# A two-layer graph network: layer one's turns written out, layer two's weights scaled and composed earlier

## The chip, the cores and the metric

The kernel runs on 1 core of one Trainium2 chip. The metric is the device time of one execution in microseconds (us); the figure compared is the median over runs.

## The reference

The input is a graph with 3125 nodes of 160 features (64 scalars and 32 three-vectors) and 103125 edges, sorted by the node that they point to. Two layers follow each other. Each normalises the node features (`h = max(layernorm(x), 0)`), gathers `h` of each edge's source node, forms a message from it and the edge's four attributes, sums the messages of each target node, and adds the result to `x`.

```python
# layer one (edge_scalars: 64 per edge, fc_w1, fc_w2: the edge's own weights)
w = silu(edge_scalars @ fc_w1 * c) @ fc_w2 * c          # 224 weights for each edge
m = products of w, (h @ lin1)[src] and the edge's attributes e0, e1
agg = segment_sum(m, dst)                               # to the target nodes
pre = (h @ sc) + (agg @ lin2)                           # scalars and vectors
x = x + [silu(pre_s[:64]), sigmoid(pre_s[64:96]) * pre_v]
# layer two (no weights of the edge's own)
m = h[src] and the edge's attributes, times W1..W5
x = x + relu(segment_sum(m, dst) @ (Ws, Wv))
```

Layer two's W1..W5 and its output weights Ws, Wv are linear, one after the other, so the kernel multiplies them into one set of planes ("composes" them) before it needs them.

## The kernel before

**Tiling.** Nodes lie in 25 tiles of 128. Edges lie in tiles of 128, 7 tiles to a group, 116 groups, 4 groups to a *turn*, 29 turns (`ITERS`) in a layer. A group's place in its turn is `o`, 0 to 3; the group's number is `s`.

**A group of layer one.** The synchronisation engine SP loads the edge features (`load_feat`). TensorE multiplies them with fc1 (`hidden`, L1216), ScalarE applies silu (L920), TensorE multiplies with fc2 (`edge_weights`, L1230). VectorE builds the selection matrices of the group (`select`, L996 and L1000), multiplies the edge weights with the gathered rows `g` (`products`, L1087 to L1105, in two halves h=0 of 4 tiles and h=1 of 3 tiles), and TensorE sums them into a window of 32 target nodes (`aggregate`, L1266). VectorE turns the sums (`turn`, L1112), TensorE multiplies them with the layer's output weights once a turn (`lin2`, L1304), ScalarE copies, VectorE adds into the accumulator at a place read from memory (`accumulate`, L1118 and L1133).

**Where the rows `g` come from.** Most tiles are gathered by POOL, one indirect transfer for each tile (`gather`, L871 to L897). A buffer of `g` is used again one turn later, so a group's gathers wait for the products (layer one) or the aggregation (layer two) of the same group of the turn before. Some tiles are found instead by comparing node numbers on VectorE (L1016, L1051) and multiplying the match with the node table on TensorE (L1287, L1294; joined at L1035, L1060): 2 tiles a turn in layer one, 4 or 5 in layer two. One tile in two of three turns is brought row by row, 128 small transfers with addresses read from memory, by SP (the first of the two) and ScalarE's queue (the second), `fetch_rows`, L779.

**Order of the turns.** `stages` (L732) calls an engine's `stage` for every group. Turns 0 and 1 are written out, turns 2 to 25 are a hardware loop over 8 periods of 3 turns, turns 26 to 28 are written out again. TensorE, VectorE and ScalarE use it in both layers. SP has a loop of its own; POOL's code is written out over all turns. Around all turns lies one more loop (`passes`), run once with these inputs.

**The head.** The node features are normalised and transformed, the table of rows is written to memory in six pieces (L379), POOL gathers the first 7 tiles (L393). SP's last transfers are a load of edge features (L380), the store of `first_rows`, which waits for `first_ready`, and the four transfers of layer two's weights `pair`, `pair_k`, `wout`, `wout_k` (L383 to L386). VectorE's last work of the head is `vector_self`: scaling `big0_sb` (L552), seven copies of TensorE's sums (L555), and the split of the node table in two halves of precision (L558).

**Between the layers.** TensorE transposes layer one's sums tile by tile (L1356), ScalarE makes sigmoid gates (`gate`, L1375), VectorE forms the gated values and the next layer norm's statistics (L1405 to L1421), POOL adds (L1457). VectorE and ScalarE normalise (L1431, L349), SP writes the second table (L1468), the table is split (L1388, L1390, L1443), VectorE computes window indices (L531 to L535). Then VectorE scales layer two's weights (L1448, L1449), TensorE composes them into 5 planes (L1365), ScalarE copies the planes (L1394), casts the first named rows (L935, L941), and VectorE's first comparison of layer two (L1051) follows.

The loop that the change takes away from layer one, as the code has it:

```python
with eng.Fori(0, PERIODS - 1) as k:
    e = eng.snap(PERIODS * r + k)
    for p in range(PERIOD):
        it = eng.snap(PERIOD * k + (LEAD + p))
        f = eng.snap(q + it)
        for o in range(UNROLL):
            stage(f, it, o, None, p, e, k)
```

Of the kernel before, what the change touches and what calls it, by code (L numbers as in the profile page):

```python
# [64 lines left out]


# [23 lines left out]
ROW_TILES = (2, 2)  # L90
PARTS = (48, 48, 32)
# [10 lines left out]
def build(nc, x, node_vec, x_node, src_idx, src_rows0, src_rows1, src_by_row, node_id, dst_idx, edge_sh, edge_feat, ident, iota, lin_sc, lin_sc_scale,  # L102
# [8 lines left out]
    with ctx:  # L111
# [250 lines left out]
        def sync_head(sp):  # L362
# [18 lines left out]
            sp.wait_ge(first_ready, RAW)  # L381
            sp.dma_start(first_rows, g[:, 0:RAW, :].rearrange("p t c -> p (t c)")).then_inc(first_out, 16)
# [3 lines left out]
            sp.dma_start(wout_k[:], l1_out_scale).then_inc(pair_in, 16)  # L386
            sp.sem_inc(first_back, 1)
# [162 lines left out]
        def vector_self(dve):  # L550
            dve.wait_ge(big0_in, 32)
            nc.vector.tensor_tensor(big0_sb[:], big0_sb[:], big0_k, ALU.mult).then_inc(big0_ready, 1)  # L552
            for j, at in enumerate(CHUNK_N):
                dve.wait_ge(sc_done[1], j + 1)
                nc.vector.tensor_copy(acc0[:, 1, at], sums[0:S_OUT, SC_BANK[1][j], 0:at.stop - at.start]).then_inc(sc_ready[1], 1)  # L555
            dve.wait_ge(rows_out, 16 * len(HEAD_PIECES))
            dve.wait_ge(upper0_ready, 2)
            nc.vector.tensor_tensor(split0[:, 0, :, :], H, split0[:, 1, :, :].bitcast(F32), ALU.subtract).then_inc(split0_ready, 1)  # L558
            dve.wait_ge(sc_ready[0], len(CHUNK_N))
            dve.wait_ge(pad_clear, 1)  # L560
            dve.wait_ge(edges_in, 48)
            dve.wait_ge(turns_set, 1)
# [87 lines left out]
        def edge_layer(layer):  # L650
# [81 lines left out]
            def stages(eng, r, stage, last):  # L732
# [4 lines left out]
                q = eng.snap(ITERS * r)  # L737
                e = eng.snap(PERIODS * r + 0) - 1
# [176 lines left out]
            def scalar(act):  # L915
# [30 lines left out]
                def row_part(f, it, o, s, p, e, k):  # L946

                    if ROW_TILES[layer] < 2 or o >= UNROLL or p < -1 or (p == PERIOD - 1 and s is not None):
                        return
# [400 lines left out]

        def tensor_mid(pe):
            for t in range(NT):
                if t >= BANKS:
                    pe.wait_ge(val_ready, t - BANKS + 1)
                for r in range(2):
                    last = nc.tensor.transpose(banks[:, t % BANKS, r * S_OUT:(r + 1) * S_OUT], acc0[:, r, t * P:(t + 1) * P],  # L1356
                                               ident_sb[0:S_OUT, 0:S_OUT])
                last.then_inc(node0_done, 1)
            pe.wait_ge(val_ready, NT)
            pe.wait_ge(weights_ready, 1)  # L1360
            for m in range(PLANES[1]):
                if m >= BANKS:
                    pe.wait_ge(comp_copied, m - BANKS + 1)
                for c in range(2):
                    last = nc.tensor.matmul(banks[:, m % BANKS, 0:D], pair[:, 2 * m + c, :], wout[:, c, :],  # L1365
                                            start=(c == 0), stop=(c == 1))
                last.then_inc(comp_done, 1)
            pe.wait_ge(comp_copied, PLANES[1])

        def scalar_mid(act):  # L1370
# [8 lines left out]
            for t in range(NT):  # L1379
                gate(t)  # L1380
            root(act, parts[0], 0, var1_step, root1_done)
# [10 lines left out]
            for m in range(PLANES[1]):  # L1392
                act.wait_ge(comp_done, m + 1)
                nc.scalar.activation(big1_sb[:, m, :], banks[:, m % BANKS, 0:D], ACT.Copy).then_inc(comp_copied, 1)  # L1394

        def vector_mid(dve):
# [50 lines left out]
            dve.wait_ge(pair_in, 64)  # L1447
            nc.vector.tensor_tensor(pair[:], pair[:], pair_k[:], ALU.mult)  # L1448
            nc.vector.tensor_tensor(wout[:], wout[:], wout_k[:], ALU.mult).then_inc(weights_ready, 1)  # L1449
# [258 lines left out]
```

## Time and profile before

| | |
|---|---|
| median of 3 runs | 1861.78 us (1860.4 to 1862.68) |
| profiled execution | time 1865.19 us, span 1863.4 us |
| busy in the span | PE 1714.3 us (92%), DVE 1685.2 us (90%), POOL 1339.0 us (72%), ACT 171.4 us (9%) |
| head | 0 to about 50 us |
| layer one | about 50 to 982 us |
| between the layers | about 982 to 1028 us |
| layer two and the end | about 1028 to 1863 us |

Names of the profile: PE is TensorE, PEld its weight loads, DVE VectorE, ACT ScalarE, POOL GpSimd, SP the synchronisation engine; a q behind an engine's name is its queue of instructions (transfers and register work). In a timeline a row is: start in us, duration in us, engine, line, operation, written tile and read tiles, shapes, count; in brackets the idle time of the engine just before it and what ended it. "issue" is idle time that nothing in the profile releases. Time in the span is counted from the first instruction.

### The profile page before, as it was taken

The numbers are of one execution on the slowest core, as the hardware profiler recorded it, in microseconds if no ns is written. First come the engines' busy times: TensorE is split into PE (matmuls) and PEld (weight loads), VectorE is DVE, ScalarE is ACT, GpSimd is POOL, SyncE is SP. The second block draws the span as 40 slices with busy tenths as digits, with TensorE's granted clock in tenths as the row PEclk, the third lists the DMA queues.
The fourth block names the chain that finished last, engine by engine and source line by source line (L and its number), as shares of the span: only waits on it lengthen the run. The fifth ranks groups of instructions, "written<-read, shape, count | busy, mean of one in ns | idle before, by whom it ended". The sixth has DMA issues, their size and how long they took to land.

```text
span 1863.4 us, 57341 instructions
## 1 busy us (share of the span) xinstructions
PE 1714.3 (92%) x15973; PEld 1488.8 (80%) x15973; DVE 1685.2 (90%) x3031; ACT 171.4 (9%) x359; POOL 1339.0 (72%) x1424
## 2 busy tenths in 40 slices
PE   8999899989898989999983899999999999999997
PEld 6677676777676767777752899999999999999997
DVE  7999899989999999999988988989898989889896
ACT  6100000000000000000005000000000000000000
POOL 4777777777777777777755777777777777777774
PEclk9899999999999999999995999999999999999999
DMA  8344443443434343434422333333333333333333
GB/s 278 105 106 108 108 110 96 107 106 98 118 91 110 102 109 103 108 91 116 112 75 86 78 84 76 83 75 84 82 76 80 83 75 82 75 81 83 74 84 90
DMA packets 109737, 181.03 MB, mean 97 GB/s; under 512 B 30072, under 2 KB 74480, under 8 KB 109248
## 3 DMA queue, kind: packets, MB, share of 16 engines
q0 software_dynamic: 66672, 113.88, 25.6%
q1 hardware_dynamic: 35592, 60.39, 10.4%
q10 hardware_dynamic: 7112, 2.94, 0.7%
q8 instruction: 106, 1.74, 0.4%
q14 instruction: 255, 2.09, 0.4%
HBM read 170.37 MB, written 6.72 MB: 95 GB/s over the span
## 4 chain that ended last, share of the span: by engine, by line
DVE 36%; PE 28%; issue 23%; ACTq 6%; DVEq 6%; DMA 1%; ACT 0%; POOL 0%; POOLq 0%
PE w_ps L1294 10%; DVE arena L1093 10%; DVE arena L1087 6%; DVE match L1051 5%; ACTq L779 5%; PE sums L1266 3%; PE sums L1270 3%; DVEq L1118 3%; PE sums L1304 3%; DVE mixed L996 3%; PE w_ps L1230 3%; DVE turned L1112 2%; PE hid_ps L1216 2%; DVE arena L1101 2%; DVE sel L1000 1%
## 5 line engine op out<-in xcount | busy, mean ns | idle before, releaser
L894 POOL DMA_INDIRECT g<-node_table,src x1382 | 1314.3, 951 | 462.1 <-issue 405.9
L1294 PE MATMUL w_ps<-split,match 128*128 128x320 f32 x3325 | 531.4, 318 | 7.9 <-DVE match L1051 7.4
L1294 PEld LDWEIGHTS w_ps<-split,match 128*128 128x128 f32 x3325 | 504.0, 193 | 12.0 <-DVE match L1051 12.0
L1051 DVE TENSOR_TENSOR match<-hid_ps,node_id_sb 128x3200 fp32r<-128x3200 f32 x105 | 361.4, 3456 | 6.9 <-ACT hid_ps L935 6.9
L1093 DVE TENSOR_TENSOR arena<-w_ps,g 128x384 f32<-128x384 f32 (+3 forms) x693 | 296.7, 455 | 2.0 <-DMA g<-node_table 1.3
L1266 PEld LDWEIGHTS sums<-arena,sel 128*32 128x32 f32 x6448 | 203.8, 111 | 116.5 <-DVE sel L1000 57.9
L1230 PE MATMUL w_ps<-fc_sb,arena 64*128 64x224 f32 x1612 | 226.9, 382 | 56.2 <-DVE arena L1087 29.5
L1000 DVE TENSOR_TENSOR sel<-mixed,sh 128x896 f32<-128x896 f32 x232 | 251.5, 1084 | 27.2
L1270 PE MATMUL sums<-g,sel 128*128 128x160 f32 x1612 | 241.5, 300 | 24.0 <-DMA g<-node_table 21.9
L1266 PE MATMUL sums<-arena,sel 128*32 128x160 f32 x6448 | 245.8, 303 | 18.0 <-DVE g L1035 17.9
L1270 PEld LDWEIGHTS sums<-g,sel 128*128 128x128 f32 x1612 | 227.2, 190 | 26.6 <-DMA g<-node_table 24.1
L1230 PEld LDWEIGHTS w_ps<-fc_sb,arena 64*128 64x128 f32 x1612 | 167.4, 193 | 100.2 <-DVE arena L1087 56.0
L1287 PE MATMUL sums<-split,match 128*128 128x320 f32 x1350 | 212.6, 313 | 0.0
L1287 PEld LDWEIGHTS sums<-split,match 128*128 128x128 f32 x1350 | 198.4, 188 | 13.6 <-issue 13.6
L1016 DVE TENSOR_TENSOR match<-mixed,node_id_sb 128x3200 fp32r<-128x3200 f32 x54 | 188.1, 3484 | 0.9
L1087 DVE TENSOR_TENSOR arena<-w_ps,g 128x256 f32<-128x256 f32 x462 | 155.6, 376 | 0.0
L1216 PE MATMUL hid_ps<-arena,fc_sb 128*128 128x512 f32 x232 | 136.2, 670 | 1.8 <-issue 1.8
L920 ACT ACTIVATE arena<-hid_ps 128x512 f32<-128x512 f32 x116 | 69.4, 598 | 740.7 <-PE hid_ps L1216 553.2
L996 DVE TENSOR_TENSOR mixed<-mixed,rel 128x224 f32<-128x224 f32 x232 | 89.4, 386 | 37.3 <-issue 30.2
L1112 DVE STREAM_TRANSPOSE turned<-sums 128x160 f32<-128x160 f32 x232 | 78.3, 338 | 26.0 <-PE sums L1304 23.1
L1051 DVE TENSOR_TENSOR match<-mixed,node_id_sb 128x3200 fp32r<-128x3200 f32 x28 | 97.8, 3492 | 1.0
L1060 DVE TENSOR_REDUCE g<-w_ps 128x160 f32<-128x320 f32 x133 | 62.5, 476 | 17.6 <-PE w_ps L1294 17.6
(113 smaller groups left out, 793.0 us busy)
## 6 DMA issues: line engine op xcount, KB each, us to landing
g<-node_table SPq DMA_DIRECT2D x2304, 0.6 KB
g<-node_table ACTq DMA_DIRECT2D x2304, 0.6 KB
arena<-edge_feat_dram SPq DMA_DIRECT2D x60, 512.0 KB
g<-node_table,src POOLq DMA_INDIRECT x1382
named<-src_rows_dram SPq DMA_DIRECT2D x30, 320.0 KB
named<-src_rows_dram SPq DMA_DIRECT2D x30, 128.0 KB
X<-x_dram SPq DMA_DIRECT2D x5, 400.0 KB, 6.5
sh<-edge_sh_dram SPq DMA_DIRECT2D x1, 1624.0 KB, 9.2
```

The costliest lines, as they stand in the source:

```text
L894: nc.gpsimd.indirect_dma_start(out=g[:, slot(p, u, j), :], out_offset=None, in_=table[layer], in_offset=bass.IndirectOffsetOnAxis(ap=src[: ...
L1000: nc.vector.tensor_tensor(sel[:, o % 2, 0:n, :].rearrange("p t (k n) -> p t k n", k=4), hot[:, 0:n, :].unsqueeze(2).to_broadcast([P, n, 4, ...
L1016: nc.vector.tensor_tensor(match0[:], wanted0[:, i, :].unsqueeze(1).to_broadcast(wide), node_id_sb[:].unsqueeze(2).to_broadcast(wide), ALU. ...
L1051: nc.vector.tensor_tensor(match[MATCH_OF[i]][:], wanted_of[i].unsqueeze(1).to_broadcast(wide), node_id_sb[:].unsqueeze(2).to_broadcast(wid ...
L1087: return nc.vector.tensor_tensor(blocks(at), w[:, :, h * S_CH:(h + 1) * S_CH].rearrange("p t (m c) -> p t m c", m=2), rows[:, :, 0:S_CH].r ...
L1093: nc.vector.tensor_tensor(blocks(at), w[:, :, 2 * S_CH + j * V_CH:2 * S_CH + (j + 1) * V_CH].unsqueeze(2).to_broadcast([P, n, m, V_CH]), r ...
L1216: nc.tensor.matmul(hid_ps[:], fc1_sb[:], feat[:, half, within * HID:(within + 1) * HID], start=True, stop=True).then_inc(hid_done, 1)
L1230: last = nc.tensor.matmul(w_ps[:, h, part[2 * h + j] - a, 0:W_N], hid[at, o % 2, (2 * h + j) * P:(2 * h + j + 1) * P], fc2_sb[at, :], tile ...
L1266: last = nc.tensor.matmul(sums[at, o % 2, 0:width].rearrange("p (m n) -> p m n", n=WIN), sel[:, o % 2, j, at], row, tile_position=(0, k * ...
L1270: last = nc.tensor.matmul(sums[:, o % 2, 0:D], sel[:, o % 2, j, :], g[:, slot(p, o % UNROLL, j), :], **first_last)
L1287: last = nc.tensor.matmul(found_at, match0[:, t, :], split0[:, :, t, :], start=(t == 0), stop=(t == NT - 1))
L1294: last = nc.tensor.matmul(banks[:, BANK_OF[i], 0:2 * D], match[MATCH_OF[i]][:, t, :], split[:, t, :], start=(t == 0), stop=(t == NT - 1))
```

## The change

1. `stages` gets a branch for layers listed in `WRITTEN_OUT`, here layer one alone: all 29 turns are written out in the code of TensorE, VectorE and ScalarE, with the turn's number known when the code is made. SP keeps its loop, POOL's code is as it was.
2. SP issues the four transfers of layer two's weights ahead of the wait for `first_ready`.
3. VectorE scales these weights in the head, in `vector_self` behind `big0_sb`, no longer between the layers.
4. TensorE composes a plane after the transposes of tiles 4, 8, 12, 16 and 20 of the stage with the gates, in the two banks of `sums` by turns; ScalarE copies a plane two tiles later, between two gates.
5. The condition in `row_part` that leaves out the last turn is written in another way, with the same effect.

```diff
+COMPOSED_AT = (4, 8, 12, 16, 20)
+WRITTEN_OUT = (0,)
@@ sync_head
             load_feat(sp, 1, 1)
-            sp.wait_ge(first_ready, RAW)
-            sp.dma_start(first_rows, g[:, 0:RAW, :].rearrange("p t c -> p (t c)")).then_inc(first_out, 16)
             sp.dma_start(pair[:], l1_pair).then_inc(pair_in, 16)
             sp.dma_start(pair_k[:], l1_pair_scale).then_inc(pair_in, 16)
             sp.dma_start(wout[:], l1_out).then_inc(pair_in, 16)
             sp.dma_start(wout_k[:], l1_out_scale).then_inc(pair_in, 16)
+            sp.wait_ge(first_ready, RAW)
+            sp.dma_start(first_rows, g[:, 0:RAW, :].rearrange("p t c -> p (t c)")).then_inc(first_out, 16)
@@ vector_self
             nc.vector.tensor_tensor(big0_sb[:], big0_sb[:], big0_k, ALU.mult).then_inc(big0_ready, 1)
+            dve.wait_ge(pair_in, 64)
+            nc.vector.tensor_tensor(pair[:], pair[:], pair_k[:], ALU.mult)
+            nc.vector.tensor_tensor(wout[:], wout[:], wout_k[:], ALU.mult).then_inc(weights_ready, 1)
@@ stages
                 q = eng.snap(ITERS * r)
+                if layer in WRITTEN_OUT:
+                    for it in range(ITERS):
+                        f = eng.snap(q + it)
+                        k, p = divmod(it - LEAD, PERIOD) if it >= LEAD else (-1, it - LEAD)
+                        e = eng.snap(PERIODS * r + max(k, 0)) - (it < LEAD)
+                        for s in range(UNROLL * it, UNROLL * (it + 1) if it < ITERS - 1 else last):
+                            stage(f, it, s - UNROLL * it, s, p, e, k)
+                    return
@@ row_part
-                    if ROW_TILES[layer] < 2 or o >= UNROLL or p < -1 or (p == PERIOD - 1 and s is not None):
+                    if ROW_TILES[layer] < 2 or o >= UNROLL or p < -1 or isinstance(it, int) and it == ITERS - 1:
@@ new functions
+        def compose(pe, m):
+            if m == 0:
+                pe.wait_ge(weights_ready, 1)
+            if m >= 2:
+                pe.wait_ge(comp_copied, m - 1)
+            for c in range(2):
+                last = nc.tensor.matmul(sums[:, m % 2, 0:D], pair[:, 2 * m + c, :], wout[:, c, :], start=(c == 0), stop=(c == 1))
+            last.then_inc(comp_done, 1)
+
+        def composed(act, m):
+            act.wait_ge(comp_done, m + 1)
+            nc.scalar.activation(big1_sb[:, m, :], sums[:, m % 2, 0:D], ACT.Copy).then_inc(comp_copied, 1)
@@ tensor_mid, in the loop over the 25 tiles
+                if t in COMPOSED_AT:
+                    compose(pe, COMPOSED_AT.index(t))
@@ tensor_mid, behind it
-            pe.wait_ge(weights_ready, 1)
-            for m in range(PLANES[1]):
...
-                last.then_inc(comp_done, 1)
@@ scalar_mid
             for t in range(NT):
                 gate(t)
+                if t - 2 in COMPOSED_AT:
+                    composed(act, COMPOSED_AT.index(t - 2))
...
-            for m in range(PLANES[1]):
-                act.wait_ge(comp_done, m + 1)
-                nc.scalar.activation(big1_sb[:, m, :], banks[:, m % BANKS, 0:D], ACT.Copy).then_inc(comp_copied, 1)
@@ vector_mid
-            dve.wait_ge(pair_in, 64)
-            nc.vector.tensor_tensor(pair[:], pair[:], pair_k[:], ALU.mult)
-            nc.vector.tensor_tensor(wout[:], wout[:], wout_k[:], ALU.mult).then_inc(weights_ready, 1)
```

## Rows read from the trace of the kernel before

**Rows 1.** Timeline, VectorE, first selection of turns 2, 5, 6 and 26.

```profile
114.57 0.40 DVE L996 TENSOR_TENSOR mixed<-mixed,rel 128x224 f32<-128x224 f32 x1 [0.33 <-PE sums L1266]
...
213.12 0.40 DVE L996 TENSOR_TENSOR mixed<-mixed,rel 128x224 f32<-128x224 f32 x1 [3.64 <-issue]
...
244.81 0.40 DVE L996 TENSOR_TENSOR mixed<-mixed,rel 128x224 f32<-128x224 f32 x1 [0.18 <-PE sums L1266]
...
897.17 0.40 DVE L996 TENSOR_TENSOR mixed<-mixed,rel 128x224 f32<-128x224 f32 x1
```

**Rows 2.** Timeline, TensorE, at a return of the loop.

```profile
206.98 1.77 PE L1230 MATMUL w_ps<-fc_sb,arena 64*128 64x224 f32 x14 [3.07 <-issue]
```

**Rows 3.** Busy times by stretch: turn 26 of layer one; three turns of layer two.

```profile
core 0: us, PE busy (x) PEld busy (x) DVE busy (x) ACT busy (x) POOL busy (x), PEclk, DMA share, GB/s
897.17:928.20 31.03, 29.39 (x355) 22.79 (x355) 30.55 (x70) 2.77 (x5) 23.41 (x26) 1.00 0.39 108
1146.32:1232.47 86.15, 83.03 (x579) 82.30 (x579) 77.53 (x80) 3.54 (x9) 65.09 (x70) 0.98 0.32 81
```

**Rows 4.** Timeline, POOL, layer one; the last is its last gather.

```profile
349.19 0.95 POOL L894 DMA_INDIRECT g<-node_table,src  x1 [0.74 <-issue]
...
415.91 0.94 POOL L894 DMA_INDIRECT g<-node_table,src  x1 [3.23 <-DVE arena L1087]
...
961.53 0.95 POOL L894 DMA_INDIRECT g<-node_table,src  x1 [0.30 <-issue]
```

**Rows 5.** Waits from 311 to 897 us: total, times, longest.

```profile
POOL g L894 <- DVE arena L1087: 18.8, 18, 3.2
```

**Rows 6.** Page, transfers: KB each, median us to landing.

```profile
wout_k<-l_out_scale_dram SPq DMA_DIRECT2D x1, 160.0 KB, 8.5
...
arena<-x_node_dram,src POOLq DMA_INDIRECT x7, 3.7
```

**Rows 7.** Timeline, VectorE, products of group 113, second half.

```profile
963.16 0.71 DVE L1093 TENSOR_TENSOR arena<-w_ps,g 128x288 f32<-128x288 f32 x2
```

**Rows 8.** Timelines of the head: SP, VectorE, POOL.

```profile
31.10 0.47 SPq L315 DMA_DIRECT2D arena<-edge_feat_dram  x1
...
39.05 1.16 DVE L552 TENSOR_TENSOR big_sb<-big_sb,arena 128x960 f32<-128x960 f32 x1
43.82 0.69 DVE L555 COPY arena<-sums 96x512 f32<-96x512 f32 x1 [3.61 <-PE sums L613]
...
39.76 1.27 POOL L894 DMA_INDIRECT g<-node_table,src  x1 [0.30 <-issue]
...
50.10 4.27 POOL L894 DMA_INDIRECT g<-node_table,src  x1 [0.30 <-issue]
```

**Rows 9.** Timelines between the layers: VectorE, TensorE, ScalarE.

```profile
1018.94 0.21 DVE L535 CAST place_i<-place 1x116 int32<-1x116 f32 x1
1019.18 1.49 DVE L1448 TENSOR_TENSOR pair<-pair,pair_k 128x1280 f32<-128x1280 f32 x1
...
1027.97 10.29 DVE L1051 TENSOR_TENSOR match<-hid_ps,node_id_sb 128x3200 fp32r<-128x3200 f32 x3 [6.89 <-ACT hid_ps L935]
...
1021.22 4.75 PE L1365 MATMUL w_ps<-wout,pair 128*128 128x160 f32 x20 [23.12 <-DVE wout L1449]
...
1022.67 0.30 ACT L1394 ACTIVATE nodes<-w_ps 128x160 f32<-128x160 f32 x1 [8.89 <-PE w_ps L1365]
...
1027.34 0.60 ACT L935 ACTIVATE hid_ps<-named 128x512 f32<-128x512 int32 x1 [1.02 <-issue]
```

**Rows 10.** Timeline, ScalarE, a gate.

```profile
985.90 0.34 ACT L1375 ACTIVATE sig<-w_ps,a_col 128x96 f32<-128x96 f32 x1 [0.30 <-DVE val L1408]
```

**Rows 11.** Chain of work that ended last, 1019 to 1021 us: start, us, what.

```profile
1020.09 0.05 DVEq L1043
```

**Rows 12.** Timelines of layer two: POOL early, POOL's last gather, TensorE's last aggregation.

```profile
1047.12 0.94 POOL L894 DMA_INDIRECT g<-node_table,src  x1 [3.11 <-PE sums L1270]
...
1841.17 0.95 POOL L894 DMA_INDIRECT g<-node_table,src  x1 [0.30 <-issue]
...
1845.44 2.44 PE L1270 MATMUL sums<-g,sel 128*128 128x160 f32 x16 [1.45 <-DVE sel L1000]
```

More of the change, by code:

```diff
@@ L1358, in tensor_mid @@
                 last.then_inc(node0_done, 1)
+                if t in COMPOSED_AT:
+                    compose(pe, COMPOSED_AT.index(t))
             pe.wait_ge(val_ready, NT)
-            pe.wait_ge(weights_ready, 1)
-            for m in range(PLANES[1]):
[L1362 to L1366, printed above, removed]
-                last.then_inc(comp_done, 1)
             pe.wait_ge(comp_copied, PLANES[1])
```

## The prediction, made before the changed kernel was run

> **What bounds the kernel now.** I read the page for the order of the stages, then the timeline of VectorE (DVE) at the starts of turns, then POOL's, then the stretch between the layers, then the ends of both layers. A turn is 4 groups. In layer one the selection of a turn's first group (L996) marks the turn on DVE. The 24 turns 2 to 25, which the old loop ran, take 897.17 - 114.57 = 782.6 us; a plain one inside the loop takes 31.7 (213.12 to 244.81), and the row at 213.12 shows 3.64 us of idle time that nothing releases [rows 1]. Seven such rows lie some 98 us apart, at each return to the loop's top; TensorE has its own at the same return, 3.07 us at 206.98 [rows 2]. Check: 24 x 31.70 = 760.8, which leaves 21.8 for 7 returns, 3.1 each. Turn 26, already straight code before the change, takes 31.03 with the clock granted in full (1.00, so 2.4 GHz) and DVE busy 30.55 of it [rows 3]. So layer one is bound by DVE, with TensorE close behind (29.39).
>
> The reader must see a third engine too. POOL starts a gather every 1.25 us (busy 0.95, then 0.30 of issue), and from 60 to 347 us it does so with no gap at all. Only later does it wait: in the 586 us that the row covers, 18 waits on DVE's products are 18.8 us, of which 18 x 0.30 is the usual issue time; one is the 3.23 at 415.91 [rows 4, 5]. By the code (gather, L871) a period of three turns has 84 tiles less 6 that are found by matching and 2 brought row by row: 76 gathers, 76 x 1.253 = 95.2 us. The loop's period was 98.1 us; three straight turns are 93.1. **POOL is the next bound.**
>
> Layer two's period of three turns (86.15 us) is TensorE's, busy 83.03 of it [rows 3]; POOL's is 68 gathers, 85.2 us, nearly as long.
>
> **The change, step by step.** *Written-out turns, VectorE and TensorE.* Removed: 7 returns and the loop's own arithmetic, (31.70 - 31.03) a turn. Without other limits the 24 turns take 24 x 31.03 = 744.7, 37.9 less. Straight code could in turn stall on fetching. Against it: DVE's straight stretches in this trace (50 to 212 us, 802 to 975) have no such gap, and POOL's code was always written out over all 29 turns and runs 287 us unbroken. I take no stall; the bound above is one return's price, 3.1 us, in every turn. ScalarE's edges lie in its idle time: nothing.
>
> A page has another price for the returns. By the rows a return costs 3.1 us on the path. The Trainium skill (Advanced Engine Details and Errata, Control Flow Timing) gives some 0.11 us for a compare-and-branch; by that the seven would be worth 0.8 us instead of 21.8, and the straight code 16.9 us instead of 37.9. This trace disagrees with it here.
>
> *What POOL leaves of it.* POOL can only close its gaps. Against its cadence of 1.253 the avoidable ones are five of 2.9 to 2.5 us (as at 415.91), together 13.3, and six of 0.42 (as at 349.19), together 2.5: 15.8 us. The other two, at 39.8 and 50.1, stay. So its last gather of the layer moves from 961.53 to 945.7 [rows 4]. What follows it keeps some slack today. Group 114 has 7 gathers and 115 one, so the last of group 113 starts 8 x 1.253 before 961.53, at 951.5. An indirect gather lands 3.7 us after its start by the only rows that show it, at the head [rows 6]: 955.2. DVE uses it at 963.16 [rows 7], 8.0 us later. Groups 112 and 114 have 11.3 and 8.8. So the layer's end can come 15.8 + 8.0 = 23.8 us sooner, not 37.9. Followed group by group: POOL is 7 to 9 us behind its earliest start at turn 2, falls back 2.1 us in each period, DVE first waits for a gather near turn 17 and runs at 31.7 a turn from there. A straight turn of 31.5 instead of 31.03 would give the same end.
>
> *Scaling in the head.* The four weight transfers leave SP some 6 us earlier, behind the load at 31.10 [rows 8]. The last took 8.5 us to land [rows 6]; issued near 33.6 it is there by 42.1, and earlier if it meets less traffic. The multiplications (1.49 at 1019.18 [rows 9], and 0.48 by the row after it) follow big0's, which ends at 40.2. DVE idles there until 43.82 [rows 8]. So they end between 42.2 and 44.1: at most 0.3 us late, taken up by the 0.2 to 0.3 that DVE waits for TensorE at each next copy. The store of first_rows, now behind them, is issued when first_ready comes, as before, and POOL needs it only in turn 1: nothing. But they cost POOL something. Beside big0's 1.16 us multiplication one gather took 1.27 instead of 0.95, and beside split0's 4.31 us subtraction one took 4.27 [rows 8]. For 1.97 us more of the same kind the bounds are 0.3 and 2.0; I take 1.0, and since POOL is the bound it is paid in full: layer one gives **22.8**.
>
> The Trainium skill says so too (GPSIMD Engine Reference, Key points): VectorE instructions with two SBUF inputs contend with GpSimd for SBUF. If both multiplications held POOL all the time it would be 2.0 us and layer one 21.8; the row at 39.76, held for 0.3 of a 1.16 us overlap at most, says less.
>
> *Composition beside the gates.* TensorE's 20 passes took 4.75 us at 1021.22 [rows 9], 0.95 per plane at the slow clock. The gate stage is paced by DVE at 0.64 a tile; ScalarE's sigmoid (0.34) ends about 1.06 us before DVE uses it, and idles 0.30 between two [rows 10]. A plane holds TensorE's next transposes back by 0.95 + 0.25 - 0.64 = 0.56 us, the copy (0.30) holds the next sigmoid back by 0.1. Both lie inside 1.06: nothing. If that cover were gone, 5 x 0.6 = 3 us.
>
> *The stretch it leaves.* Today: index columns done at 1019.16, multiplications, TensorE, copies, ScalarE's casts at 1027.34, first comparison (L1051) at 1027.97. Without them DVE enters the layer at once; its queue reached the comparison's wait at 1020.09 with the multiplication running beside it. ScalarE is idle for 8.89 us before 1022.67, so from 1013.8; its casts can be done by 1016. The first comparison starts at 1020.1: **7.9** sooner [rows 9, 11].
>
> *Does layer two hand it on?* POOL's start (1012.83) does not move against the table's stores. It runs on to 1043.06 and then idles 3.11 [rows 12]; that 2.8 it can recover. The remaining 5.1 us are lag, on top of 3 to 7 today. The least slack of any group's last gather before the TensorE stage that reads it is 7.4 us (group 11) until the very end, and becomes 2.3. At the end, 1841.17 + 3.7 against the last pass near 1847.3 (the end of the row at 1845.44) is 2.4 [rows 12]; with TensorE 7.9 sooner and POOL, never waiting, 7.2 sooner (2.8 + 4.4 of gaps after 1415), 1.7 stays. All 7.9 arrive. The row waits in each period (2.2 to 3.0 us for ScalarE's row loads) follow TensorE and stay.
>
> **Sum.** 22.8 + 7.9 = 30.7. The profiled execution has span 1863.4 and time 1865.19; it becomes 1834.5, span 1832.7. The median shown is 3.4 lower, 1861.78: forecast **1831.1**.
>
> **Rivals.** *POOL does not bind* (chance 0.07). Gathers come faster or land in time; then 37.9 + 7.9 = 45.8, 1816.0. For it: no gather wait in layer one now. Against: the cadence of 1.25 us holds in both layers, whether POOL is behind or not.
> *Layer two is led by its gathers* (0.12). Then only 2.8 of the 7.9 arrive: 1836.2. It begins where gathers land 2.3 us later than 3.7, and takes all 5.1 from 7.4 us later. For it: POOL's start does not move. Against: the head's landings.
> *The composition is not covered* (0.08): gates 3 us longer, 1834. For it: five planes at 0.95. Against: the 1.06 of slack.
> *Slower* (0.03). Written-out code stalls on fetching. Place: DVE and TensorE in turns 2 to 25. Price: 3.1 us in every turn is 74.4, against 45.8 gained: 1890. It decides from 45.8 / 24 = 1.9 us a turn. By the unbroken straight stretches this is unlikely.
> The Trainium skill (Runtime: NRT & Kernel Launch, Instruction fetch mechanics) speaks for the straight code: fetching ahead is sequential and a taken branch out of the window breaks it.
> *The forecast* (0.70): 22.8 and 7.9, within a few us.
>
> **Range and chances.** Gather landing of 2.0 instead of 3.7 gives 1.7 more, POOL's contention 0.7 more, to 1828.7; landing later, 2.0 for contention, a slower clock on entering layer two, each about 1, to 1835. With the second and third rivals and a part of the first: 1823 to 1840. 0.2% (3.7 us) is what a measurement here can tell. Every case but the slow one is faster: faster 0.95, same 0.02, slower 0.03.
>
> **What would show it.** Right: no 3 us issue gaps on DVE or TensorE before 1000; turns of 31.0 in the first half and near 31.7 later; POOL's waits on DVE near zero; DVE waits for gathers late in layer one; layer one's last gather near 946; the first L1051 some 2.4 us after the last L1443 ends. Wrong: regular issue gaps in straight turns; gathers stretched beyond 0.95; waits of TensorE for gathers at other places of layer two than the last tile of each third turn; a gate stage above 0.64 a tile.

## The result, and the profile after

The changed kernel takes a median of 1831.28 us (1829.36 to 1834.22, 4 runs) against 1861.68 for the kernel before on the same chip: a ratio of 0.984, 95% interval 0.982 to 0.986, 30.4 us less. The forecast was 1831.1. The profiled execution of after has span 1832.4 and time 1834.22.

Lines below are those of the new code: `gather` is L909, the products L1102 and L1108, the first comparisons of layer two L1066, `aggregate` with gathered rows L1285, `lin2` L1319, `compose` L1373.

**Layer one, straight turns.** Timeline of VectorE, first selections of turns 2, 3 and 4, the loop's first turns before [rows 1]:

```profile
117.26 0.40 DVE L1011 TENSOR_TENSOR mixed<-mixed,rel 128x224 f32<-128x224 f32 x1
148.28 0.40 DVE L1011 TENSOR_TENSOR mixed<-mixed,rel 128x224 f32<-128x224 f32 x1
179.30 0.40 DVE L1011 TENSOR_TENSOR mixed<-mixed,rel 128x224 f32<-128x224 f32 x1
```

A turn takes 31.02 us, as turn 26 did before (31.03, [rows 3]), and no idle "issue" time of 3 us [rows 1, 2] is left in the layer. Up to turn 17 turns take 31.0 to 31.4. Then VectorE meets POOL; the waits from 56 to 952 us, of them those that touch a gather (total, times, longest), and the first and one of the longest of them in VectorE's timeline:

```profile
POOL g L909 <- issue: 213.5, 700, 0.3
DVE arena L1108 <- DMA g<-node_table,src: 13.5, 13, 1.6
POOL g L909 <- DVE arena L1102: 4.6, 15, 0.3
```

```profile
622.47 0.89 DVE L1108 TENSOR_TENSOR arena<-w_ps,g 128x384 f32<-128x384 f32 x2 [0.69 <-DMA g<-node_table,src]
...
688.66 0.72 DVE L1108 TENSOR_TENSOR arena<-w_ps,g 128x288 f32<-128x288 f32 x2 [1.55 <-DMA g<-node_table,src]
...
941.30 0.72 DVE L1108 TENSOR_TENSOR arena<-w_ps,g 128x288 f32<-128x288 f32 x2 [1.54 <-DMA g<-node_table,src]
```

The roles are exchanged. Before, POOL waited up to 3.2 us for VectorE's products [rows 5] and VectorE for no gather. Now POOL's waits on the products are 0.3 at most, which is its usual issue time, and VectorE waits 13 times for a gather, from 622 us (turn 18) on. Where it waits, a turn takes up to 32.7. The page's chain of work that ended last says the same in one line:

```profile
DVE 24%; issue 23%; PE 22%; POOL 20%; ACTq 6%; DVEq 3%; DMA 2%; ACT 0%; POOLq 0%
```

POOL had 0% of the chain before and has 20% now.

**The head.** The multiplications by VectorE, and POOL beside them (timelines, to be held against [rows 8]):

```profile
42.61 1.49 DVE L558 TENSOR_TENSOR pair<-pair,pair_k 128x1280 f32<-128x1280 f32 x1
44.01 0.48 DVE L559 TENSOR_TENSOR wout<-wout,wout_k 128x320 f32<-128x320 f32 x1
46.30 0.69 DVE L562 COPY arena<-sums 96x512 f32<-96x512 f32 x1 [1.80 <-PE sums L620]
...
42.16 1.36 POOL L909 DMA_INDIRECT g<-node_table,src  x1 [0.30 <-issue]
43.82 1.10 POOL L909 DMA_INDIRECT g<-node_table,src  x1 [0.30 <-issue]
```

The multiplications lie in VectorE's idle time: 1.80 us of the 3.61 are still idle behind them. The first copy is 2.5 us later than before, but so is POOL's first gather (35.88, was 33.50), which waits for the table's stores, and SP issues those ahead of every changed line. In `e2_composed_only`, below, whose head has the same code, that gather starts at 33.02, so most of the delay is this execution's and not the change's.

**Between the layers.** VectorE's timeline, for [rows 9], and POOL's first gather of layer two:

```profile
997.69 0.21 DVE L539 CAST place_i<-place 1x116 int32<-1x116 f32 x1
998.83 10.29 DVE L1066 TENSOR_TENSOR match<-hid_ps,node_id_sb 128x3200 fp32r<-128x3200 f32 x3 [0.92 <-DVE place_i L539]
...
991.64 1.62 POOL L909 DMA_INDIRECT g<-node_table,src  x1 [9.53 <-DMA node_table<-nodes]
```

From the cast to the first comparison are 1.14 us, before 1027.97 - 1018.94 = 9.03 [rows 9]: 7.9 less, to the tenth what was predicted. POOL's first gather stays where it was, 6.05 us ahead of that cast (before 6.1).

**The end of layer two.** TensorE's last two aggregation rows, the `lin2` behind them, and POOL's last gather; the last two rows of [rows 12] answer to them:

```profile
1809.68 1.35 PE L1285 MATMUL sums<-g,sel 128*128 128x160 f32 x8 [1.46 <-DVE sel L1015]
1813.11 2.50 PE L1285 MATMUL sums<-g,sel 128*128 128x160 f32 x8 [2.07 <-DMA g<-node_table,src]
1816.05 3.64 PE L1319 MATMUL sums<-turned,nodes 128*80 128x128 f32 x20 [0.44 <-DVE turned L1127]
...
1811.71 0.95 POOL L909 DMA_INDIRECT g<-node_table,src  x1 [0.30 <-issue]
```

Before, the last gather started 4.3 us ahead of TensorE's last aggregation. Now it starts 2.0 us behind it, and TensorE waits 2.07 us in the middle. This was not forecast.

### The profile page after: what moved, and what is told of

It is laid out like the page before. It is cut to its first block, busy times and chain, and to the rows that moved or that the text cites. A ratio compares the mean times of both kernels' runs of the same rounds, so it can differ in the third digit from the quotient of the medians.

```text
span 1832.4 us, 56986 instructions
## 1 busy us (share of the span) xinstructions
PE 1705.7 (93%) x15973; PEld 1483.5 (81%) x15973; DVE 1683.6 (92%) x3031; ACT 170.4 (9%) x359; POOL 1338.7 (73%) x1424
## 4 chain that ended last, share of the span: by engine, by line
DVE 24%; issue 23%; PE 22%; POOL 20%; ACTq 6%; DVEq 3%; DMA 2%; ACT 0%; POOLq 0%
POOL g L909 20%; PE w_ps L1309 10%; DVE match L1066 6%; DVE arena L1108 5%; ACTq L794 5%; PE sums L1285 3%; PE sums L1319 3%; DVE arena L1102 3%; DVE mixed L1011 2%; DVEq L1133 2%; DVE turned L1127 2%; ACTq L791 1%; DMA g<-node_table 1%; DVE g L1075 1%; DVE sel L1015 1%
## 5 line engine op out<-in xcount | busy, mean ns | idle before, releaser
L909 POOL DMA_INDIRECT g<-node_table,src x1382 | 1314.0, 951 | 441.7 <-issue 406.8
L1066 DVE TENSOR_TENSOR match<-hid_ps,node_id_sb 128x3200 fp32r<-128x3200 f32 x105 | 361.4, 3456 | 0.9 <-DVE place_i L539 0.9
L1108 DVE TENSOR_TENSOR arena<-w_ps,g 128x384 f32<-128x384 f32 (+3 forms) x693 | 297.3, 456 | 14.7 <-DMA g<-node_table,src 13.5
L1281 PEld LDWEIGHTS sums<-arena,sel 128*32 128x32 f32 x6448 | 203.4, 110 | 109.8 <-DVE sel L1015 56.6
L1285 PE MATMUL sums<-g,sel 128*128 128x160 f32 x1612 | 242.4, 301 | 24.6 <-DMA g<-node_table 20.4
L1285 PEld LDWEIGHTS sums<-g,sel 128*128 128x128 f32 x1612 | 227.9, 191 | 27.6 <-DMA g<-node_table 22.6
L1245 PEld LDWEIGHTS w_ps<-fc_sb,arena 64*128 64x128 f32 x1612 | 162.4, 189 | 88.3 <-DVE arena L1102 68.4
L1102 DVE TENSOR_TENSOR arena<-w_ps,g 128x256 f32<-128x256 f32 x462 | 155.7, 377 | 0.0
L1066 DVE TENSOR_TENSOR match<-mixed,node_id_sb 128x3200 fp32r<-128x3200 f32 x28 | 97.8, 3492 | 1.0
L943 ACT ACTIVATE lin_sb<-sums 96x256 f32<-96x256 f32 (+1 forms) x58 | 22.0, 380 | 573.3 <-PE sums L1319 469.2
```

What stands on the lines that cost most here:

```text
L909: nc.gpsimd.indirect_dma_start(out=g[:, slot(p, u, j), :], out_offset=None, in_=table[layer], in_offset=bass.IndirectOffsetOnAxis(ap=src[: ...
L1066: nc.vector.tensor_tensor(match[MATCH_OF[i]][:], wanted_of[i].unsqueeze(1).to_broadcast(wide), node_id_sb[:].unsqueeze(2).to_broadcast(wid ...
L1102: return nc.vector.tensor_tensor(blocks(at), w[:, :, h * S_CH:(h + 1) * S_CH].rearrange("p t (m c) -> p t m c", m=2), rows[:, :, 0:S_CH].r ...
L1108: nc.vector.tensor_tensor(blocks(at), w[:, :, 2 * S_CH + j * V_CH:2 * S_CH + (j + 1) * V_CH].unsqueeze(2).to_broadcast([P, n, m, V_CH]), r ...
L1245: last = nc.tensor.matmul(w_ps[:, h, part[2 * h + j] - a, 0:W_N], hid[at, o % 2, (2 * h + j) * P:(2 * h + j + 1) * P], fc2_sb[at, :], tile ...
L1281: last = nc.tensor.matmul(sums[at, o % 2, 0:width].rearrange("p (m n) -> p m n", n=WIN), sel[:, o % 2, j, at], row, tile_position=(0, k * ...
```

## The experiments

Medians are in us. The kernel before, on the same chip, took 1860.29 beside the first four experiments, 1859.73 beside the next four, 1859.16 beside both_layers_fewer_two, 1861.42 beside the two with earlier rows, and 1860.54 beside the last.

### One half of the change each

`e1_written_only` is the kernel before with points 1 and 5 of the change alone, `e2_composed_only` is after with the loop back in layer one:

```diff
-WRITTEN_OUT = (0,)
+WRITTEN_OUT = ()
```

> Layer one's turns written out, nothing else of the change (weights scaled and composed between the layers as before). By my theory (POOL's gathers bound layer one once the loop is gone) the gain is 15.8 + 8.0 = 23.8 us, 1 us more than in the full change because the multiplications in the head don't hold POOL: about 1838. If the returns and the loop's arithmetic were the whole story, 37.9 us: about 1824. If the two parts of the change weren't independent, this run and the one with the composition alone would not sum to the full change's 30.4.

> The loop stays in layer one; weights are scaled in the head and composed beside the gates. Theory: 7.9 us from the stretch between the layers, all of it handed on by layer two: about 1853.8. Rival (layer two is led by its gathers, whose start doesn't move): 2.8 us, about 1859.

Measured: **1834.91** (ratio 0.986, 0.984 to 0.988), 25.4 less than before; and **1856.67** (0.998, 0.997 to 0.999), 3.6 less. They add to 29.0, within the spread of the 30.4 of both. The written-out turns bring a little more than forecast (23.8 without the multiplications in the head, 22.8 with them), the composition less than half of its 7.9. In the trace of `e2_composed_only` the first comparison is as early as in after; TensorE's timeline at its end shows where the rest went:

```profile
1828.07 1.08 PE L1285 MATMUL sums<-g,sel 128*128 128x160 f32 x6 [0.95 <-DMA g<-node_table,src]
1833.25 2.47 PE L1285 MATMUL sums<-g,sel 128*128 128x160 f32 x8 [4.10 <-DMA g<-node_table,src]
1836.86 2.50 PE L1285 MATMUL sums<-g,sel 128*128 128x160 f32 x8 [1.13 <-DMA g<-node_table,src]
```

Three waits for gathers, 6.2 us together, in a place where the kernel before has none. (The table further down has the same place in every run.)

### Fewer gathers in layer one

POOL gathers one tile less in each of turns 2 to 25 of layer one; what is computed from that tile then uses an earlier turn's rows, so these two kernels give other sums and serve for their times alone. It is done in after (`e3_after_fewer_gathers`) and in before (`e4_before_fewer_gathers`, the control):

```diff
                         others |= {TILES - 1} if u in PICKED0 and fetched(group) else set()
+                        others |= {0} if u == 1 and 2 <= it < ITERS - PERIOD else set()
```

> The changed kernel, with one gather left out in each of turns 2 to 25 of layer one (the first tile of the turn's second group; its rows are then those of an earlier turn, so part of the messages is computed from other rows). POOL's period falls from 95.2 to 91.5 us, under the 93.1 of three straight turns. If POOL is what limits layer one after the change, layer one gets 10 to 15 us shorter: 1816 to 1821, and VectorE's waits for gathers in layer one go. If POOL doesn't limit it, no change: 1831.

> The kernel before with the same gathers left out (one in each of turns 2 to 25 of layer one; part of the messages is computed from other rows). With the loop's period of 98.1 us POOL had time to spare, so both theories expect no change, within 1 us: 1861.7; POOL's waits on VectorE grow from some 22 to about 50 us. If it gets faster by several us, gathers cost VectorE or TensorE something by merely running beside them, and the run before it has to be read less this amount.

Measured: **1820.07** (0.978, 0.976 to 0.980), 11.2 below after by the medians, 9.8 when each is held against the kernel before beside it; and **1860.02** (1.000, 0.999 to 1.001), no change. The same relief is worth 10 to 11 us in after and nothing in before, so POOL's gathers are what limits the new layer one. VectorE's first selections of turns 19 and 20 in `e3_after_fewer_gathers`:

```profile
646.05 0.40 DVE L1012 TENSOR_TENSOR mixed<-mixed,rel 128x224 f32<-128x224 f32 x1
...
677.09 0.40 DVE L1012 TENSOR_TENSOR mixed<-mixed,rel 128x224 f32<-128x224 f32 x1
```

31.04 in turn 19, where after has 31.42, and 31.0 to 31.1 in all turns from 18 to 26, where after has 31.0 to 32.7. VectorE has no wait for a gather left. From the first to the last selection layer one takes 883.8 us, against 896.1 in after and 922.3 in `e4_before_fewer_gathers`: with POOL eased on both sides the straight turns are worth 38.5, and the prediction had 37.9 "without other limits".

### The price of a return, and whose return it is

`e5_two_periods`: the kernel before with two periods in the loop's body in layer one, 3 returns instead of 7.

```diff
+                if layer == 0:
+                    with eng.Fori(0, (PERIODS - 1) // 2) as kk:
+                        for half in range(2):
+                            k = eng.snap(2 * kk + half)
...
```

`e6_dve_written`: the kernel before with the turns written out for VectorE alone.

```diff
-                if layer in WRITTEN_OUT:
+                if layer in WRITTEN_OUT and eng is nc.vector:
```

> The kernel before, but layer one's loop has a body of two periods (6 turns) and runs 4 times: 3 returns instead of 7, the loop's arithmetic stays. If each return costs 3.1 us on the path, as the rows say, 4 x 3.1 = 12.4 us come off: about 1848. POOL allows it, since its avoidable gaps (15.8 us) are more. If the cost lies in the computed addresses and counters, under 2 us: about 1859. If a return costs the 0.11 us of a plain compare-and-branch, nothing measurable.

> Written out for VectorE alone; TensorE and ScalarE keep the loop in layer one. TensorE's return (3.07 us idle) comes some 6 us before VectorE's in the same turn. If the two lie one behind the other on the path, VectorE alone gives about half of the returns and its own arithmetic, 8 to 16 us: 1845 to 1852. If they hide each other, TensorE's 3 us stay on the path and VectorE alone gives only its arithmetic: 4 us or less, 1856 or more.

Measured: **1845.73** (0.992, 0.991 to 0.994), 14.0 less for four returns, 3.5 each (3.0 to 4.0 by the interval); and **1834.72** (0.986, 0.984 to 0.988), 25.0 less. The second was missed: VectorE alone brings what the three engines bring (25.0 against 25.4, each to some 3 to 4 us). TensorE keeps its returns, in `e6_dve_written`:

```profile
205.10 1.29 PE L1239 MATMUL w_ps<-fc_sb,arena 64*128 64x224 f32 x8 [3.40 <-issue]
```

In five turns they make VectorE 1.4 to 2.1 us late (33.05 instead of 31.0 in turn 5). But POOL sets when the layer ends: the last gather starts 913.1 us after the first, as in after (912.9), and VectorE, late, just waits less for it. So TensorE's part of the change is worth nothing measurable while POOL is the bound. Were POOL no bound, its price could be up to some 9 us, the sum of what those five turns are late; this wasn't tried.

### Layer two: its returns, and its gathers

`e7_both_layers` is after with layer two's turns written out too; `e8_fewer_gathers_two` is after with one gathered tile less in turns 2 to 25 of layer two; `e9_both_layers_fewer_two` has both; `e12_written_fewer_two` is `e1_written_only` with the fewer gathers. As in layer one, the kernels with fewer gathers compute from an earlier turn's rows.

```diff
-WRITTEN_OUT = (0,)
+WRITTEN_OUT = (0, 1)
@@ gather, the branch of layer two
+                        others |= {0} if u == 0 and 2 <= it < ITERS - PERIOD else set()
```

> The changed kernel with layer two written out as well. If POOL's unbroken gathers set layer two's length (655 of them at 1.25 us, 820 us from first to last in the changed kernel), the loop there is hidden: within 2 us of the changed kernel, 1829 to 1833. If TensorE and the row loads of ScalarE set it, the 7 returns there cost 2 to 3 us each: 1812 to 1818.

> The changed kernel with one gather left out in each of turns 2 to 25 of layer two (first tile of the turn's first group; part of layer two's messages is computed from other rows). The composition alone gave 3.6 us, not 7.9. If the missing 4 us are POOL's, they come now: 1825 to 1828, and TensorE's waits for POOL's gathers at the end of layer two go. If they are lost elsewhere (a slower start, TensorE's clock), no change: 1831.

> Both layers written out, and one gather left out in each of turns 2 to 25 of layer two (part of layer two's messages is computed from other rows). With POOL out of the way, what the loop costs TensorE, VectorE and ScalarE in layer two must show: 10 to 20 us under the kernel with the same gathers left out and layer one alone written out, so 1806 to 1817. If the loop is free in layer two for another reason (its returns lie beside matmuls), it equals that kernel.

> Layer one written out, weights composed between the layers as before, and one gather left out in each of turns 2 to 25 of layer two (part of layer two's messages is computed from other rows). It stands to the changed kernel with the same gathers left out (1825.4) as written-out alone stands to the full change. With POOL out of the way the composition should be worth its whole 7.9 us: this one 1833 to 1834, 1 to 2 under the kernel without the gathers left out (1834.9). If the composition is worth only 3.6 us for another reason than POOL, this one comes at 1829.

Measured: **1829.99** (0.984, 0.983 to 0.986), the same as after. **1825.38** (0.981, 0.980 to 0.982), 4.6 below `e7_both_layers` on the same chip; below after it is 5.9 by the medians and 4.0 when each is held against the kernel before beside it. **1823.83** (0.980, 0.978 to 0.983), only 1.6 (so held, 1.0) below that: a miss, layer two's returns cost almost nothing even with POOL eased. **1829.99** (0.983, 0.982 to 0.985), 4.9 (so held, 5.2) below `e1_written_only`, more than expected.

The traces show why the returns of layer two cost nothing. In after, whose layer two still has its loop, this is VectorE's first selection of turn 5 there, at a return, and the only wait that TensorE has from 1050 to 1800 us (total, times, longest), for the rows brought one by one:

```profile
1147.21 0.40 DVE L1011 TENSOR_TENSOR mixed<-mixed,rel 128x224 f32<-128x224 f32 x1 [0.68 <-issue]
```

```profile
PE sums L1285 <- DMA g<-node_table: 20.4, 9, 2.8
```

VectorE's longest idle "issue" time in that stretch is 0.74 us, where layer one had over 3, and TensorE, which is busy nearly all the time in this layer [rows 3], has none.

TensorE's end in `e8_fewer_gathers_two` is what the prediction had in mind for after:

```profile
1810.68 2.44 PE L1286 MATMUL sums<-g,sel 128*128 128x160 f32 x16 [1.46 <-DVE sel L1016]
1813.57 2.41 PE L1320 MATMUL sums<-turned,nodes 128*80 128x128 f32 x20 [0.44 <-DVE turned L1128]
```

No wait for a gather, and the last aggregation ends 2.44 us after its start instead of 5.93. TensorE's clock differs as well; windows of after over its last aggregation, over the 6 us in which the clock is down, and over what follows, and of `e8_fewer_gathers_two` over what follows (engine times, then the clock granted, the share of the transfer engines, GB/s):

```profile
1809.00:1816.00 7.00, 3.86 (x16) 3.21 (x16) 1.96 (x7) 0.00 (x0) 2.84 (x3) 0.70 0.20 47
1812.00:1818.00 6.00, 4.45 (x17) 4.05 (x18) 1.47 (x6) 0.00 (x0) 0.66 (x1) 0.50 0.12 27
1816.00:1832.00 16.00, 10.56 (x70) 10.10 (x70) 7.96 (x20) 0.38 (x1) 0.00 (x0) 0.61 0.42 129
```

```profile
1813.50:1828.00 14.50, 8.66 (x70) 8.20 (x70) 7.88 (x21) 0.38 (x1) 0.00 (x0) 0.71 0.47 142
```

In after the granted clock is 0.50 (1.2 GHz) from 1812 to 1818 us: it falls within 1 us of the start of the wait of 2.07. The 8 passes behind the wait take 2.50 us, the 8 ahead of it 1.35, and the 20 of `lin2` 3.64 instead of 2.41. So the last aggregation is 3.5 us longer, 2.1 of it the wait and 1.4 the lower clock, and 1.2 more are lost behind it.

### A third bound of layer two

TensorE still waits in each period for rows that SP and ScalarE's queue bring (the nine waits above). `e10_rows_earlier` issues layer two's rows earlier in the period; `e11_rows_earlier_fewer_two` has fewer gathers besides.

```diff
-SHARES = ((12,) * 8 + (12, 12, 8, 0),) * 2
+SHARES = ((12,) * 8 + (12, 12, 8, 0), (12, 12, 12, 24, 12, 12, 12, 24, 8, 0, 0, 0))
```

> The changed kernel; ScalarE loads the rows of layer two's row-by-row tile in other shares (24 instead of 12 in two stages, none in the two stages just before the tile is used). TensorE's wait of 2 to 3 us for them in each period should go. If POOL sets layer two's length, as the runs so far say, the time stays within 2 us: 1829 to 1833, with TensorE waiting for POOL's gathers instead. If TensorE and the row loads set it, 8 x 2.3 = 18 us less: 1813.

> The same shares, and one gather left out in each of turns 2 to 25 of layer two (part of layer two's messages is computed from other rows). The kernel with the fewer gathers alone took 1825.4. If TensorE's wait for the row loads is what is left to gain there once POOL is out of the way, up to 18 us less: 1808 to 1815. If it was free time anyway, 1825.

Measured: **1866.18** (1.002, 1.001 to 1.004) and **1866.03** (1.003, 1.001 to 1.004), both 35 us slower than after. The expectation failed, and since fewer gathers don't help, it is not POOL. Whether the row waits of after bound it is not shown by this pair, because the change made a larger wait elsewhere. ScalarE's queue and TensorE behind it, in `e10_rows_earlier`, and TensorE's waits from 1040 us on:

```profile
1146.06 16.74 ACTq L794 DMA_DIRECT2D g<-node_table  x36
1165.54 0.38 ACT L943 ACTIVATE lin_sb<-sums 80x256 f32<-80x256 f32 x1 [20.68 <-issue]
...
1166.17 4.01 PE L1285 MATMUL sums<-g,sel 128*128 128x160 f32 x14 [5.51 <-ACT lin_sb L943]
```

```profile
PE sums L1285 <- ACT lin_sb L943: 45.6, 10, 5.9
```

36 row loads hold ScalarE's queue for 16.74 us (0.47 each), and its copy of TensorE's sums stands behind them in order. TensorE waits 4.6 us for that copy in each of ten places. The rows' own waits are gone: a wait was removed by making a larger one.

## Why the prediction was right in its sum and wrong in one step

*What POOL leaves of the straight turns.* Right in place and kind: VectorE's first wait for a gather comes in turn 18 (forecast near 17), `e3_after_fewer_gathers` and its control show POOL as the bound. The size was 22.8, or 23.8 without the 1.0 for the head; `e1_written_only`, which has no multiplications in the head, gives 25.4. The term that was mis-sized is the slack of group 113's last gather. From POOL's first gather to its last, layer one shrank by 15.2 us (961.53 - 33.50 before, 948.73 - 35.88 after), the 15.8 less 1.0 of the forecast within 0.4. The slack used up was put at 8.0 with a landing time of 3.7 us, that of a gather from another table in the head. The real one is 2.6: group 113's last gather starts 8 x 1.253 before 948.73, at 938.7, and VectorE's wait for it ends at 941.30. With 2.6 the slack is 9.1 and layer one 24.9 (23.9 with the head's 1.0). The remaining 0.5 us is well within the interval of the measurement (some 3.7 us either way).

*The rival "POOL does not bind"* fell: `e3_after_fewer_gathers` shows what it would have looked like. *The rival "slower"* fell too: no fetching stall stands anywhere in the straight turns. The price of a return was 3.1 from rows and 3.5 by `e5_two_periods`. (Of the "seven such rows" on VectorE six are idle time put down to nothing; the seventh, 3.14 us at 704.05, is put down to TensorE's sums. The count of returns and the price stand.) The 0.11 us of the Trainium skill (Advanced Engine Details and Errata, Control Flow Timing) would have made four returns worth 0.4 us; the run gave 14.0. Its rule on fetching (Runtime: NRT & Kernel Launch, Instruction fetch mechanics) fits layer one: straight code of the whole layer runs without a stall, each taken return has one. In layer two the loop returns as often, and from 1050 to 1800 us of after no "issue" time over 0.74 us stands on VectorE and none on TensorE, so a taken return alone is not what costs 3 us. The Trainium skill ties the stall there to a target outside the window that is held. A loop's body has some 1065 matmuls in layer one (3 x 355) and 579 in layer two [rows 3]; whether that sets the two apart was not tried, and what the stall waits for no run here shows.

*The head* was put at nothing, with 1.0 us of contention on POOL. POOL's gathers beside the multiplications took 1.36 and 1.10 instead of 0.95, 0.6 more together, of which 0.3 went beside big0's alone before [rows 8]; the one beside the split took 5.38 instead of 4.27. That VectorE's instructions with two SBUF inputs hold GpSimd back is what the Trainium skill says (GPSIMD Engine Reference, Key points); the trace agrees, in part of the overlap only. Over the profiled executions of all kernels the head up to the first selection is 53.5 to 54.9 us without the composition and 54.4 to 56.6 with it. That leaves up to 1 us for it, too little to be told from the spread.

*The gates.* Forecast nothing; from the first transpose to the first normalised tile it is 19.92 us against 19.63, 0.3 more, where the rival "the composition is not covered" wanted 3. The cover held.

*The stretch between the layers* ends 7.9 us sooner, as worked out. *"All 7.9 arrive"* is the step that failed: 3.6 arrived. Its working took the slack at the end of layer two, and the 4.4 us of gaps that POOL could recover after 1415 us, from one profiled execution. In us from POOL's first gather of layer two, worked out from the timelines of every run but the two with earlier rows. The second column is the start of TensorE's last aggregation but one (1841.85 in before, 1806.08 in after), the third its waits for indirect gathers from there on:

| | last gather | TensorE's row | waits for gathers |
|---|---|---|---|
| *not composed early* | | | |
| before, as profiled | 828.3 | 829.0 | 0 |
| e1_written_only | 826.1 | 821.9 | 0.6 |
| e4_before_fewer_gathers | 824.3 | 822.7 | 0 |
| e5_two_periods | 823.8 | 821.6 | 0 |
| e6_dve_written | 826.1 | 824.2 | 0 |
| *composed early* | | | |
| after | 820.1 | 814.4 | 2.1 |
| e2_composed_only | 822.3 | 812.5 | 6.2 |
| e3_after_fewer_gathers | 822.1 | 812.9 | 6.0 |
| e7_both_layers | 820.2 | 812.7 | 5.3 |
| *fewer gathers in layer two* | | | |
| e8_fewer_gathers_two (composed early) | 815.7 | 816.4 | 0 |
| e9_both_layers_fewer_two (composed early) | 811.7 | 812.1 | 0 |
| e12_written_fewer_two (not) | 820.3 | 820.8 | 0 |

In the execution that the prediction read, layer two's turns 2 to 26 took 715.6 us. In the profiled executions of all the others in the table they took 705.6 to 709.9, whether composed early or not. TensorE was 5 to 7 us later there than in the four other kernels with the same layer two, and POOL's larger gaps late in the layer are put down to TensorE's sums, for which it waited; the four others lack them. Usually POOL has one avoidable gap, 3.2 to 4.2 us (`e4_before_fewer_gathers` waits 3.92 at the place of the 3.11 in [rows 12]), and its last gathers land less than 2 us before they are needed: there the last but one starts at 1837.81, so by 2.6 us of landing its rows are there at 1840.4, and TensorE takes them in the middle of its last aggregation, near 1842.2 (an estimate). In after POOL runs from 991.64 to 1811.71 with no gap over 0.32 us; 655 gathers in 820.07 us, 1.254 apart. So TensorE's gain ended at POOL's last gathers: with the early composition TensorE comes to that row 7 to 12 us sooner than without, and then waits in all four kernels; without it only one of five waits, 0.6 us; with fewer gathers none does. That is the second rival, "layer two is led by its gathers", which gave 2.8 and had 0.12.

The medians of the eased kernels don't prove it by themselves. Fewer gathers bring 4.0 to 5.9 us with the early composition and 4.9 to 5.2 without it, where the explanation wants more with it.

What stays open: with POOL eased, the composition should bring its whole 7.9. `e8_fewer_gathers_two` against `e12_written_fewer_two`, the same pair with and without it, gives 4.6 by the medians and 3.8 when each is held against the kernel before beside it. Each has an interval of some 2.6 us either way, so this fits 3.6 and leaves 7.9 at the edge. In their profiled executions TensorE is 6.3 us ahead at turn 2 and 4.5 at turn 27, without a wait for a gather between; the spread from execution to execution is as large. Whether a second claimant takes a part is not settled.

*The sum.* Layer one brought 2.6 more and the stretch 4.3 less than forecast, so 1831.1 met 1831.28 by two errors of opposite sign. The mechanism of layer one was right; that the total fits to 0.2 us is luck.

## What to carry to other kernels

Before pricing the removal of a stall, measure the cadence of the next engine and how far behind its earliest start it runs: here VectorE could give 38 us, POOL let 25 through, and TensorE's share was worth nothing. Read a slack of a few us from more than one profiled execution, because a stretch that ran slow in the one at hand shows gaps and slack that the code does not have. Time given to the consumer ahead of a long stretch only arrives if the producer's start moves too; the place to look is the last transfer of the stretch.

## What the runs showed of the hardware

- A return of the hardware loop in layer one, with a body of three turns (some 98 us), leaves VectorE and TensorE idle for 2.8 to 3.7 us each; straight code of 29 turns showed no such gap.
- With a body twice as long a return costs the same. VectorE's three in `e5_two_periods` are 3.1 to 3.4, TensorE's 3.5 to 3.7:

```profile
309.40 0.40 DVE L1007 TENSOR_TENSOR mixed<-mixed,rel 128x224 f32<-128x224 f32 x1 [3.25 <-issue]
```

- Not every return has that gap. Layer two's loop has as many returns, and between 1050 and 1800 us of after no idle "issue" time is over 0.74 us on VectorE and none stands on TensorE. Written out with POOL eased they bring 1.6 us in all by the medians (`e8_fewer_gathers_two` against `e9_both_layers_fewer_two`), which is within their spread.
- An indirect gather of 128 rows from the node table is there 2.6 us after its start (layer one's end in after), and POOL starts one each 1.25 us, behind or not.
- In after, TensorE's granted clock fell from 1.00 to 0.50 within the first 1 us of a wait of 2.07 us that came 1.35 us of work behind one of 1.46, and the `lin2` there took half as long again: 3.64 us for 20 passes instead of 2.41. In `e8_fewer_gathers_two`, with the wait of 1.46 alone, `lin2` took 2.41.
